# Depthwise 3x3 convolutions of a four-layer block: one or two of the nine taps go to ScalarE and GpSimd

## What is computed

```python
# layer 0 (a state-space block with an MLP; h is the normed input)
c1 = dwconv2d(h, cpe1_w, cpe1_b);  x1 = h + c1          # then layer norm, SSD, projection
c2 = dwconv2d(x2, cpe2_w, cpe2_b); x3 = x2 + c2         # then layer norm, MLP
# layer 1 (a selective scan in four directions, 384 channels)
xc = silu(conv(xa, conv_w) + conv_b)                    # xa: projection of the normed input
# layers 2 and 3
x = x + (conv(gn(x), w) + b)
```

## Time and profile before

| | us |
|---|---|
| runs, median of 3 | 30871.11 |
| runs, lowest and highest | 30860.43, 30885.85 |
| the profiled execution's own time | 30867.51 |
| its span (first to last instruction in the trace) | 30864.8 |
| VectorE busy | 25385.2 |
| TensorE busy | 25968.3 |
| GpSimd busy | 20760.7 |
| ScalarE busy | 19655.2 |

### The profile page before, as it was taken

One profiled execution on the slowest core, in us unless ns is written; L12 is line 12 of the kernel. 1 busy time (PEld: TensorE's weight loads), 2 busy tenths in 40 slices (PEclk: granted clock), 3 DMA queues, 4 the chain that ended last, 5 costly groups with the idle time before them and its releaser, 6 DMA issues. The chain is left out here.

```text
span 30864.8 us, 300702 instructions
## 1 busy us (share of the span) xinstructions
PE 25968.3 (84%) x78624; PEld 11973.3 (39%) x78624; DVE 25385.2 (82%) x28488; ACT 19655.2 (64%) x36856; POOL 20760.7 (67%) x9038
## 2 busy tenths in 40 slices
PE   8888888888788888888878888788888888878888
PEld 3344333443334433344333443334433344333443
DVE  6799867998679986799867998679986799867998
ACT  4677546775467754677546775467754677546775
POOL 2689626896268962689626896268962689626896
PEclk8999989999899998999989999899998999989999
DMA  0111101111011110111101111012110111101111
GB/s 7 48 57 59 44 8 48 57 58 44 9 48 58 58 44 8 47 58 59 43 9 48 57 59 44 8 48 58 58 44 8 48 58 58 44 8 48 58 58 44
DMA packets 844554, 1330.07 MB, mean 43 GB/s; under 512 B 226176, under 2 KB 243456, under 8 KB 839680
## 3 DMA queue, kind: packets, MB, share of 16 engines
q1 hardware_dynamic: 842752, 1309.85, 14.6%
HBM read 1241.87 MB, written 67.63 MB: 42 GB/s over the span
## 5 line engine op out<-in xcount | busy, mean ns | idle before, releaser
L1572 PE MATMUL ps<-arena,ident 128*128 128x512 f32 x24576 | 11920.7, 613 | 807.5 <-DVE arena L1770 807.5
L1793 DVE TENSOR_TENSOR_SCAN arena<-ps,arena 128x512 f32<-128x512 f32 x6912 | 8626.1, 1269 | 410.5 <-ACT ps L1653 410.5
L1476 POOL TENSOR_TENSOR arena<-arena 128x1536 f32<-128x1536 f32 x2320 | 8012.7, 3454 | 940.3 <-DVE arena L1793 939.7
L1793 DVE TENSOR_TENSOR_SCAN arena<-arena,ps 128x512 f32<-128x512 f32 x5376 | 6651.2, 1261 | 249.5 <-PE ps L1590 136.6
L1572 PEld LDWEIGHTS ps<-arena,ident 128*128 128x128 f32 x24576 | 4391.0, 195 | 5382.9 <-issue 3062.2
L1737 POOL TENSOR_TENSOR arena<-arena 128x1536 f32<-128x1536 f32 x1536 | 5300.2, 3459 | 562.2 <-ACT arena L1624 562.2
L1653 ACT ACTIVATE ps<-arena 128x512 f32<-128x512 f32 x6912 | 4738.2, 686 | 1020.3 <-DVE arena L1793 1006.0
L1770 DVE TENSOR_TENSOR arena<-arena,ps 128x512 f32<-128x512 f32 x6144 | 4059.9, 661 | 598.8 <-PE ps L1581 562.0
L1637 ACT ACTIVATE scaled<-arena,cols 128x384 f32<-128x384 f32 x7168 | 3975.2, 603 | 183.2 <-PE ps L1590 183.2
L1590 PEld LDWEIGHTS ps<-ident,scaled 128*128 128x128 f32 x21504 | 2604.0, 143 | 3472.8 <-DVE arena L1793 1784.8
L1653 ACT ACTIVATE arena<-arena 128x512 f32<-128x512 f32 x5376 | 3750.5, 717 | 83.2 <-PE ps L1572 83.1
(11 more groups left out here) (184 smaller groups left out, 31846.8 us busy)
## 6 DMA issues: line engine op xcount, KB each, us to landing
arena<-rows SPq DMA_DIRECT2D x3904, 256.0 KB, 3.4
spare<-rows SPq DMA_DIRECT2D x520, 256.0 KB, 4.0
arena<-x SPq DMA_DIRECT2D x16, 1536.0 KB, 13.6
x<-arena SPq DMA_DIRECT2D x16, 1536.0 KB, 10.7
arena<-x SPq DMA_DIRECT2D x64, 384.0 KB, 4.3
out<-arena SPq DMA_DIRECT2D x64, 384.0 KB, 3.0
rows<-xd SPq DMA_DIRECT2D x264, 64.0 KB, 1.6
arena<-L_conv_fc_w SPq DMA_DIRECT2D x16, 576.0 KB, 5.5
```

Source lines behind the costliest of these rows:

```text
L1476: return nc.gpsimd.tensor_tensor(three(dbu[:, no % DB, :]), du[:, par, :, :], each, ALU.mult)
L1572: nc.tensor.matmul(m.ps[:, t, :], m.ident[:, :], x, start=False, stop=(no == order.last_sum(b, t))).then_inc(at["y_mm"], 1)
L1793: nc.vector.tensor_tensor_scan(flip(hs[:, g % HS, here]), flip(decays), flip(adds), carry[:, k, N2 * n + t:N2 * n + t + 1], ALU.mult, ALU. ...
```

## The change

`conv3x3` gets a tuple `beside` of one or two taps that neither TensorE nor VectorE does, and a table `pe_share` of how many taps TensorE does in each step. For the taps beside, ScalarE multiplies the pixels by the tap's weight into a ring of four steps of side buffers in SBUF (`products`, up to four steps ahead of the evictions). GpSimd adds the two products of a step into one (`gather`, one step ahead), or the residual onto the one product where there is a residual, and after ScalarE's eviction adds that to the step in SBUF. Taps 7 and 1 are beside in the first three convolutions (`TWO`, `WIDE`), tap 7 in the last two (`ONE`). In layer 1 the eviction no longer applies the Silu; ScalarE does it in place once GpSimd has added. The lines removed and added:

```diff
--- before.py
+++ after.py
@@ -28,7 +28,9 @@
 MLP = 4 * C
 NM = MLP // 128
 CENTRE = 4
+AHEAD = 4
 PE_TAPS = (CENTRE, 3, 5, 1)
+TWO, ONE, WIDE = dict(beside=(7, 1), pe_share=(0, 3, 3, 3, 3, 3, 3, 3)), dict(beside=(7,), pe_share=(0, 3, 3, 4, 4, 3, 3, 4)), dict(beside=(7, 1), pe_share=(0, 3, 3, 3, 3, 3, 3, 3, 3, 3, 3, 3))
 SLOT = L
 SLOTS = 12
 LN_EXP = "natural_log_exp_and_others"
@@ -234,12 +236,13 @@
 
     NAMES = ("taps_loaded", "centre")
 
-    def __init__(self, m, n, parts, weight, bias, own=False, slot=SLOTS):
+    def __init__(self, m, n, parts, weight, bias, own=False, slot=SLOTS, side=None):
         self.m, self.n, self.parts, self.weight, self.bias, self.own = m, n, parts, weight, bias, own
         m.start(slot)
         self.w = m.take(n, 9, parts=parts)
         self.b = m.take(n, parts=parts)
         self.diag = m.take(n * len(PE_TAPS), parts, parts=parts)
+        self.side = m.slots(side, 2, parts).rearrange("p a (b c l) -> p (a b) c l", b=2, c=2) if side is not None else None
 
     def sync(self, sp, loaded):
         nc = self.m.nc
@@ -260,19 +263,20 @@
                                         w[:, t, tap:tap + 1], None, ALU.mult)
 
 
-def conv3x3(m, src, dst, taps, residual=None, silu=False, out=None, loads=()):
+def conv3x3(m, src, dst, taps, residual=None, silu=False, out=None, loads=(), beside=(), pe_share=()):
 
     nc, n, parts = m.nc, taps.n, taps.parts
     w, bcol, diag = taps.w, taps.b, taps.diag
     steps = [(t, r) for t in range(n) for r in range(0, H, ROWS)]
     src4 = src.rearrange("p t (h w) -> p t h w", w=W)
     last = len(steps) - 1
+    side = taps.side
 
     def pe_taps(i):
-        return () if i == 0 else PE_TAPS[:3] if i <= 2 else PE_TAPS
+        return PE_TAPS[:pe_share[i]]
 
     def dve_taps(i):
-        own = [tap for tap in range(9) if tap not in pe_taps(i)]
+        own = [tap for tap in range(9) if tap not in pe_taps(i) and tap not in beside]
         return own if i else [CENTRE] + [tap for tap in own if tap != CENTRE]
 
     halved = {i: [(i, half) for half in range(2)] for i in (0, last)}
@@ -287,26 +291,62 @@
     def rows(v, t, r):
         return v[:, t, r * W:(r + ROWS) * W]
 
+    def moved(i, tap):
+
+        t, r = steps[i]
+        (ya, yb, _, _), (sa, _, _, _) = window(tap, r, r + ROWS)
+        return t, ya, yb - ya, sa
+
     def banks(i):
         return m.ps[0:parts, (2 * i) % 8:(2 * i) % 8 + 2, :]
 
-    with Stage(nc, "taps_mm", "taken", "tapped", "whole", "stored", "brought") as (taps_mm, taken, tapped, whole, stored,
-                                                                                    brought), nc.Block() as block:
+    own = len(beside)
+    with Stage(nc, "taps_mm", "taken", "tapped", "side_done", "filled", "gathered", "side_added", "silu_out", "stored", "brought") as (
+            taps_mm, taken, tapped, side_done, filled, gathered, side_added, silu_out, stored, brought), nc.Block() as block:
         @block.sync
         def _(sp):
             bring(m, sp, brought, loads)
             if out is not None:
                 for i, (t, r) in enumerate(steps):
-                    sp.wait_ge(whole, i + 1)
+                    sp.wait_ge(side_added, i + 1)
                     sp.dma_start(rows(out, t, r), rows(dst, t, r)).then_inc(stored, 16)
                 sp.wait_ge(stored, 16 * len(steps))
 
-        if residual is not None:
-            @block.gpsimd
-            def _(pool):
+        @block.gpsimd
+        def _(pool):
+            gathers = max(own - 1, 0) + (residual is not None)
+
+            def gather(i):
+
+                n, (t, r) = gathers * i, steps[i]
+                whole_side = side[:, i % AHEAD, 0, :]
+                for j, tap in enumerate(beside):
+                    t, ya, height, _ = moved(i, tap)
+                    pool.wait_ge(side_done, own * i + j + 1)
+                    if j == 0 and height < ROWS:
+                        nc.gpsimd.memset(whole_side[:, height * W:], 0.0).then_inc(filled, 1)
+                        pool.wait_ge(filled, t + 1)
+                    if j:
+                        part = whole_side[:, (ya - r) * W:(ya - r + height) * W]
+                        nc.gpsimd.tensor_tensor(part, part, side[:, i % AHEAD, j, 0:height * W], ALU.add).then_inc(gathered, 1)
+                if residual is not None:
+                    if own > 1:
+                        pool.wait_ge(gathered, n + own - 1)
+                    nc.gpsimd.tensor_tensor(whole_side, whole_side, rows(residual, t, r), ALU.add).then_inc(gathered, 1)
+
+            if own:
+                gather(0)
+                for i, (t, r) in enumerate(steps):
+                    if i < last:
+                        gather(i + 1)
+                    pool.wait_ge(taken, i + 1)
+                    if gathers:
+                        pool.wait_ge(gathered, gathers * (i + 1))
+                    nc.gpsimd.tensor_tensor(rows(dst, t, r), rows(dst, t, r), side[:, i % AHEAD, 0, :], ALU.add).then_inc(side_added, 1)
+            elif residual is not None:
                 for i, (t, r) in enumerate(steps):
                     pool.wait_ge(taken, i + 1)
-                    nc.gpsimd.tensor_tensor(rows(dst, t, r), rows(dst, t, r), rows(residual, t, r), ALU.add).then_inc(whole, 1)
+                    nc.gpsimd.tensor_tensor(rows(dst, t, r), rows(dst, t, r), rows(residual, t, r), ALU.add).then_inc(side_added, 1)
 
         @block.tensor
         def _(pe):
@@ -325,10 +365,32 @@
 
         @block.scalar
         def _(act):
+            def products(i):
+                if i >= AHEAD and own:
+                    act.wait_ge(side_added, i - AHEAD + 1)
+                for j, tap in enumerate(beside):
+                    t, _, height, sa = moved(i, tap)
+                    nc.scalar.activation(side[:, i % AHEAD, j, 0:height * W], src[:, t, sa * W:(sa + height) * W], ACT.Copy,
+                                         scale=w[:, t, tap:tap + 1]).then_inc(side_done, 1)
+
+            def through_silu(i):
+                t, r = steps[i]
+                act.wait_ge(side_added, i + 1)
+                nc.scalar.activation(rows(dst, t, r), rows(dst, t, r), ACT.Silu).then_inc(silu_out, 1)
+
+            for i in range(AHEAD):
+                products(i)
             for i, (t, r) in enumerate(steps):
                 act.wait_ge(tapped, tapped_all[i])
                 nc.scalar.activation(rows(dst, t, r).rearrange("p (a b) -> p a b", a=2), banks(i),
-                                     ACT.Silu if silu else ACT.Identity, bias=bcol[:, t:t + 1]).then_inc(taken, 1)
+                                     ACT.Silu if silu and not own else ACT.Identity, bias=bcol[:, t:t + 1]).then_inc(taken, 1)
+                if silu and own and i >= 2:
+                    through_silu(i - 2)
+                if i and i - 1 + AHEAD <= last:
+                    products(i - 1 + AHEAD)
+            if silu and own:
+                through_silu(last - 1)
+                through_silu(last)
 
         @block.vector
         def _(dve):
@@ -1956,17 +2018,17 @@
             s01, s23, s45 = m.slots(0, NH, P), m.slots(2, NH, P), m.slots(4, NH, P)
 
 
-            taps = Taps(m, NH, P, l0["cpe1_w"], l0["cpe1_b"], own=True)
+            taps = Taps(m, NH, P, l0["cpe1_w"], l0["cpe1_b"], own=True, side=10)
             group_norm(m, s01, s23, taps, load=xb)
-            taps_2 = Taps(m, NH, P, l0["cpe2_w"], l0["cpe2_b"], own=True)
+            taps_2 = Taps(m, NH, P, l0["cpe2_w"], l0["cpe2_b"], own=True, side=10)
             weights, loads = ssd_weights(m, l0)
-            conv3x3(m, s23, s45, taps, loads=loads)
+            conv3x3(m, s23, s45, taps, loads=loads, **TWO)
             ssd(m, s45, weights, taps_2)
             weights, loads = mlp_weights(m, l0)
-            conv3x3(m, s45, s23, taps_2, loads=loads)
+            conv3x3(m, s45, s23, taps_2, loads=loads, **TWO)
             mlp(m, s23, s01, weights)
 
-            taps = Taps(m, N2, 128, l1["conv_w"], l1["conv_b"], slot=8)
+            taps = Taps(m, N2, 128, l1["conv_w"], l1["conv_b"], slot=8, side=2)
             m.start(7)
             w_in = m.take(NH, D2, parts=P)
             group_norm(m, s01, s23, taps, loads=[(w_in, l1["in_proj_w"].rearrange("(t p) o -> p t o", p=P)[:, :, 0:D2])],
@@ -1974,16 +2036,16 @@
             xa, xc, y = m.slots(4, N2), m.slots(9, N2), m.slots(6, N2)
             project(m, s23, xa, w_in, s01, x1v)
             weights, loads = scan_weights(m, l1)
-            conv3x3(m, xa, xc, taps, silu=True, loads=loads)
+            conv3x3(m, xa, xc, taps, silu=True, loads=loads, **WIDE)
             selective_scan(m, xc, y, weights, rows)
             finish_scan(m, y, s01, x1v, l1)
 
-            taps = Taps(m, NH, P, l2["w"], l2["b"])
+            taps = Taps(m, NH, P, l2["w"], l2["b"], side=10)
             group_norm(m, s01, s23, taps, have_stats=True)
-            conv3x3(m, s23, s45, taps, residual=s01)
-            taps = Taps(m, NH, P, l3["w"], l3["b"])
```

(4 more changed lines are left out.)

## The result

Three runs of the changed kernel took 30607.5, 30609.1 and 30622.0 us (a fourth, at 40074.3 us with a mean granted clock of 0.67, is left out). The kernel before took 30860.4 to 30886.1 beside them, median 30878.5. The ratio is 0.9915, interval 0.9895 to 0.9934. The forecast was 30558, in a range from 30525 to 30640: the sign and the range hold, and the time is 51 us above the forecast.

The account below looks back on a forecast made before the run. The convolutions were taken as bound by VectorE; late start, TensorE's step 6, VectorE's pieces, 1.19 and GpSimd's 9.4 us tail gave 39.2 us less a sample, 313 in all: 30871 - 313 = 30558 us, range 30525 to 30640.

Parts of the forecast that it names:

- What bounds the kernel: In the five convolutions, 8.5% of the time, VectorE is the bound, with TensorE close behind and ScalarE and GpSimd nearly free.
- VectorE's new share: In a two-tile convolution, VectorE's work falls from 55.5 us to about 42 by losing taps 1 and 7.
- TensorE sets the pair (5, 6): Near a convolution's end VectorE waits for TensorE's step 6, ready 30.7 us after TensorE's late start in two-tile convolutions.
- 7.2 us of pieces: Six pieces of VectorE work between step 6 being ready and the eviction of step 5: 7.2 us.
- 1.19: From the start of step 5's eviction to GpSimd's first add behind it: 1.19 us.
- tail 9.4: At a convolution's end GpSimd has four adds and a small memset left after step 5's eviction: 9.4 us.
- ScalarE at nothing: ScalarE's two products a step, 1.13 us each, stay hidden: 3.2 us with the eviction against a step of 5.1.
- the table load: In the third convolution it moves to the first Silu, costed at nothing; at most 9 us in all.
- The late start of the first convolution: TensorE's first matmuls at the lower clock delay it by 1.9 us, 3.3 in the seventh sample, counted in full.
- Everything outside of conv3x3 stays: Barriers, SyncE's loads and all stages outside the convolutions were taken as unchanged, with no term in the sum.
- rivals 1 and 2: First: GpSimd's adds slower beside ScalarE writing what they read, 30590 to 30750 us, chance 0.09; second: see Rival 2.
- Rival 2: TensorE's full clock comes later in the convolutions; one to three us more each gives 30600 to 30680 us; chance 0.05.

Follow-up runs that it names:

- a_share: Changed kernel with TensorE doing two taps instead of three in steps 1 and 2 of the first, fourth and fifth convolutions; 30567.3 us, ratio 0.9901.
- a_gather2: Changed kernel with GpSimd's gathering adds two steps ahead of the add onto the sum instead of one; 30570.2 us, ratio 0.9902.
- a_act: Changed kernel with a further unread ScalarE product of 768 elements ahead of each product; 30696.0 us, ratio 0.995.
- a_all: a_gather2 plus a_share's first convolution, and TensorE taps (0, 3, 3, 3, 3, 4, 4, 4) in the fourth and fifth; 30504.5 us, ratio 0.9884.
- a_all_delay: a_all, but its second convolution gathers one step ahead and has a GpSimd memset of 1152 elements behind its last add; 30478.5 us, ratio 0.9879.

## Why the prediction came out as it did

- **What bounds the kernel, and VectorE's new share: right.** VectorE is at 42.35 us where 42 was worked out, and at 61.02 in the third.
- **TensorE sets the pair (5, 6), 7.2 us of pieces, 1.19, tail 9.4: right** to 0.1 us each, in the timeline above; a_share and a_gather2 show that TensorE's start and the tail are on the path, each for its price.
- **ScalarE at nothing: right**, also the table load (8 of 1.28 us, none ahead of a late eviction: the third convolution of sample 0 took 70.0 with 70.2 worked out). a_act shows where the cover ends.
- **The late start of the first convolution: too small.** I took 1.9 us from sample 0 and 3.3 from the seventh; over the eight samples of before it was 1.9 to 3.3 with 2.8 in the mean, and 2.4 to 3.5 after. That cost 0.4 us a sample against the forecast (a gain of 6.8 in place of 7.2), nearly all of it since the late start itself grew, from 2.8 to 3.1 in the mean: the clock again, and not the edit's own work. The third gained 15.2 (15.0), the others were within 0.2.
- **"Everything outside of conv3x3 stays": the step that failed.** The code did, the time didn't: 54 us came back, 33.5 of them behind the second convolution. The trace of before had part of it in sight: that stretch took 273.3 to 277.6 us with the same work in different samples, and nowhere did I ask why. The last sentence of the prediction named it as what could go wrong; it had no price and no chance. From the spread in before alone it was worth some 23 us down and 11 up; with the 271 to 280 us that the later runs show, 44 down and 34 up. That belongs in the range.
- **The range: held in part by luck.** It reached up to 30640 for rivals 1 and 2, slower adds and a late clock inside the convolutions. Neither came, but for 3 us of the first convolution's later start, and the clock outside of the convolutions used the room.
- **Rival 2** had the right engine and the wrong place: the clock inside the convolutions came as before (5 to 8 late matmuls in the first, against 4 to 7), and late in the stages behind them.

## What to carry over

A stage made shorter moves all that follows it, and where TensorE's clock goes up and down in those stages their length changes with it: look at how much an untouched stage varies between iterations of the kernel before, and put that into the range. Before a kernel is called better by a few tens of microseconds in 30000, cut both traces at the stages that were changed and at those that weren't; the first number says what the edit is worth, the second what the clock made of it. And when an engine is relieved so that its late start costs less, see that it doesn't pause instead.

## What the runs showed of the hardware

- The same MLP stretch, instruction for instruction, takes 270.7 to 280.5 us, by the instant at which it begins: counted from the start of the convolution ahead, the full clock comes at 76.6 to 76.8 us in three kernels in which that convolution takes 48.65, 49.35 and 49.64 us. In the kernel before, 1.1 us of memset ahead of it made it 3.7 us longer, and 2.0 us made it 5.3 us shorter.
- A wait of 1.94 us of TensorE inside an otherwise dense run of matmuls was followed by 7.2 us at 0.54 of its clock (a_share, fifth convolution); pauses of 2.0 us or less from the start of one matmul to that of the next were not followed by a lower clock in a_share, a_all and a_all_delay, those of 2.05 to 2.67 there were in all 13 cases. In the second and third convolution of before, 2.47 to 2.50 us never were.
- GpSimd adds of 1024 elements (2.35 us) beside VectorE taps that read one operand from SBUF and one from PSUM: the taps take 1.262 us with them and without, and an add beside a ScalarE that writes the buffers it reads takes what it took in before (2.35). The lock that the Trainium skill ("SBUF — State Buffer", section "SBUF: two separate sides") describes for two operands in SBUF isn't met here, as the prediction had it. In the second convolution the two engines are busy for 42.35 and 37.21 of the same 48.75 us, so for at least 30.8 of them together.
